# The causal layer with its key tiles in the order 0, 7, 1, 6, 2, 5, 3, 4, and its value products split by bank

## What is computed

```
x = layer_norm(hidden_states, ln1_w, ln1_b)
q = (x @ q_w + q_b) / math.sqrt(HEAD)      # 16 heads of 8 channels, 1024 tokens
k = x @ k_w + k_b
v = x @ v_w + v_b
scores = jnp.einsum('bhqd,bhkd->bhqk', q, k)
scores = jnp.where(causal, scores, neg)
attn = jax.nn.softmax(scores, axis=-1)
ctx = jnp.einsum('bhqk,bhkd->bhqd', attn, v)
```

## Time and profile before

| | |
|---|---|
| median of 3 runs | 3524.71 us (3523.38 to 3525.19) |
| profiled execution, its own time | 3526.23 us |
| its span, first to last instruction | 3524.5 us |
| TensorE busy, share of the span | 3180.8 us, 90% |
| VectorE, GpSimd, ScalarE busy | 70%, 53%, 48% |
| mean granted clock of TensorE | 0.937 of full speed |

### The profile page before, as it was taken

The page is one execution under the profiler, slowest core; times in us unless marked ns, Lnnn a source line. Parts: engine busy times, 40 slices in busy tenths (PEclk is TensorE's granted clock), DMA queues, the critical chain, the costliest instruction groups (busy, mean ns, idle before and its releaser), DMA issues. The chain is left out here.

```text
span 3524.5 us, 50933 instructions
## 1 busy us (share of the span) xinstructions
PE 3180.8 (90%) x18448; PEld 1856.2 (53%) x18448; DVE 2477.8 (70%) x4334; ACT 1689.5 (48%) x2048; POOL 1871.0 (53%) x1159
## 2 busy tenths in 40 slices
PE   5979797586448999999999999999999999999998
PEld 4757576332324555555555555555555555555445
DVE  6979798653258776877777787687777778767533
ACT  5758576243213444444444444444444444444442
POOL 3857575111222655655665565565566556556670
PEclk8989899567679999999999999999999999999998
DMA  1000000000410000000000000000000000000001
GB/s 62 1 1 1 1 1 1 12 1 1 140 22 3 1 1 1 4 1 1 1 4 1 1 4 1 1 4 1 1 1 4 1 1 2 1 1 1 1 1 35
DMA packets 20600, 28.47 MB, mean 8 GB/s; under 512 B 5124, under 2 KB 12424, under 8 KB 20232
## 3 DMA queue, kind: packets, MB, share of 16 engines
q1 hardware_dynamic: 19016, 22.09, 1.9%
q0 software_dynamic: 1344, 3.15, 0.3%
HBM read 21.56 MB, written 3.67 MB: 7 GB/s over the span
## 5 line engine op out<-in xcount | busy, mean ns | idle before, releaser
L2049 ACT ACTIVATE pair_probs<-banks 128x1024 f32<-128x1024 f32 (+1 forms) x944 | 965.5, 1026 | 1035.2 <-PE banks L1959 983.8
L2098 DVE TENSOR_REDUCE pair_peaks<-banks 128x1 f32<-128x512 f32 (+1 forms) x1800 | 1085.6, 665 | 271.4 <-PE banks L1941 257.6
L2191 POOL TENSOR_TENSOR pair_total_pool<-pair_total_pool,pair_probs 128x1536 f32<-128x1536 f32 x208 | 724.6, 3484 | 754.1 <-DVE pair_total L2112 748.9
L1982 PE MATMUL banks<-pair_probs,pair_values 128*64 128x512 f32 (+1 forms) x3776 | 872.8, 600 | 0.0
L1941 PE MATMUL banks<-pair_k_high,pair_q_high 64*128 64x512 f32 (+1 forms) x1920 | 568.0, 443 | 26.6 <-DVE pair_peaks L2091 14.0
L2180 POOL TENSOR_TENSOR pair_total_pool<-pair_total_pool,pair_probs 128x1024 f32<-128x1024 f32 x224 | 535.7, 2392 | 39.1 <-POOL pair_total_pool L2191 21.4
L2112 DVE TENSOR_TENSOR pair_total<-pair_total,pair_probs 128x512 f32<-128x512 f32 (+2 forms) x464 | 457.9, 987 | 94.5 <-ACT pair_probs L2049 69.3
L1982 PEld LDWEIGHTS banks<-pair_probs,pair_values 128*64 128x64 f32 (+1 forms) x3776 | 248.3, 136 | 472.6 <-issue 384.7
L1959 PE MATMUL banks<-pair_q_shift,pair_one_rows 64*128 64x512 f32 (+1 forms) x1888 | 475.4, 396 | 3.1 <-ACT pair_probs L2049 3.1
L1941 PEld LDWEIGHTS banks<-pair_k_high,pair_q_high 64*128 64x128 f32 x1920 | 263.1, 185 | 356.4 <-issue 211.9
L1959 PE MATMUL banks<-pair_q_high,pair_k_high 64*128 64x512 f32 (+1 forms) x1888 | 426.9, 391 | 0.0
(11 more groups left out here) (323 smaller groups left out, 3770.3 us busy)
## 6 DMA issues: line engine op xcount, KB each, us to landing
expert_w<-in_fc SPq DMA_DIRECT2D x32, 256.0 KB, 4.3
context_rows<-in_ctx SPq DMA_DIRECT2D x10, 320.0 KB, 6.4
dense_w<-in_We SPq DMA_DIRECT2D x2, 1024.0 KB, 9.2
experts_in<-expert_zeros SPq DMA_DIRECT2D x1, 1024.0 KB, 3.8
expert_b<-in_fc_b SPq DMA_DIRECT2D x2, 512.0 KB, 4.7
expert_rows<-experts_in SPq DMA_DIRECT2D x16, 64.0 KB, 2.0
experts_out<-expert_result POOLq DMA_DIRECT2D x4, 256.0 KB, 4.6
row_parameters<-in_rows SPq DMA_DIRECT2D x1, 896.0 KB, 8.4
```

The lines of the kernel that those rows point to most:

```text
L1982: last = pe.matmul(out[heads[head], :], values[0:n, ring_of(h // 2, i // 4), i % 4, heads[head]], probs_of(h, i)[0:n, head, :], start=i == ...
L2049: act.activation(probs_of(h, i)[0:n], slot(e)[0:n], ACT.Exp, scale=1.0 / 8.0).then_inc(S["expd"].sem, 1)
L2098: v.reduce_max(peaks[:, head, t, b:b + 1], fill_bank(f, head)[:, 0:width(b)], axis=AX).then_inc(S["peaked"].sem, 1)
L2191: pool.tensor_tensor(pooled[:], pooled[:], three, ALU.add).then_inc(S["pooled"].sem, 1)
```

## The change

The key tiles are taken in the order 0, 7, 1, 6, 2, 5, 3, 4. An add is split in two entries for tiles 0 to 3, one for each bank, each with its own semaphore count. The adds of a tile no longer stand behind the last unit of the next tile, but are spread between its units. The turns of the next group's queries and keys stand behind the first and the second score instead of ahead of all; the back of the group before stands behind the seventh score (in group 3 behind the first). The ring of `probs` and GpSimd's order go by the position of a tile in the new order.

```diff
+KEY_TILES = (0, 7, 1, 6, 2, 5, 3, 4)
+def banks_of(j):
+    return range(j // 4, 2)
...
-        for j in range(TT):
-            behind += [("score", g) + s for s in scores[j]]
-            if j:
-                behind.append(("add", g, j - 1))
         if g:
-            ahead.insert(min(4, len(ahead)), ("back", g - 1))
-        order += ahead[:2]
-        ahead = ahead[2:]
-        for entry in behind:
-            order.append(entry)
-            if entry[0] == "score" and ahead:
-                order.append(ahead.pop(0))
+            ahead.insert(min(6, len(ahead)), ("back", g - 1))
+        for n, j in enumerate(KEY_TILES):
+            adds = [("add", g, KEY_TILES[n - 1], bank) for bank in banks_of(KEY_TILES[n - 1])] if n else []
+            for m, piece in enumerate(scores[j]):
+                order.append(("score", g) + piece)
+                if ahead:
+                    order.append(ahead.pop(0))
+                while adds and (m + 1) * len(banks_of(KEY_TILES[n - 1])) >= len(scores[j]) * \
+                        (len(banks_of(KEY_TILES[n - 1])) - len(adds) + 1):
+                    order.append(adds.pop(0))
         order += ahead
         if g + 1 < NG:
             order.append(("shift", g + 1))
-        order += [("add", g, TT - 1), ("keep", g)]
+        order += [("add", g, KEY_TILES[-1], bank) for bank in banks_of(KEY_TILES[-1])] + [("keep", g)]
...
-                def add(g, j):
-                    wait(pe, "selected", TT * g + j + 1)
+                def add(g, j, bank):
+                    n = position[j]
+                    wait(pe, "selected", TT * g + n + 1)
                     wait(pe, "taken_scalar", last_score[g, j])
-                    if j == 0:
+                    if n == 0:
                         wait(pe, "kept", g)
-                    for bank in range(j // 4, 2):
-                        a, b = max(j * P, bank * 512), bank * 512 + 512
-                        for h in range(GROUP):
-                            last = pe.matmul(out[PART * h:PART * h + PART, bank, a - bank * 512:512],
-                                             values[:, j, g * GROUP + h, :], probs[:, j % 3, h, a - j * P:b - j * P],
-                                             start=j == 0, stop=j == 4 * bank + 3)
+                    a, b = max(j * P, bank * 512), bank * 512 + 512
+                    for h in range(GROUP):
+                        last = pe.matmul(out[PART * h:PART * h + PART, bank, a - bank * 512:512],
+                                         values[:, j, g * GROUP + h, :], probs[:, n % 3, h, a - j * P:b - j * P],
+                                         start=n == 0, stop=j == [c for c in KEY_TILES if bank in banks_of(c)][-1])
```

More of the change, by code:

```diff
@@ L908, in causal_order @@
         ahead = [("queries", g + 1), ("keys", g + 1)] + [("fill", g + 1) + f for f in fills] if g + 1 < NG else []
-        behind = []
-        for j in range(TT):
-            behind += [("score", g) + s for s in scores[j]]
-            if j:
-                behind.append(("add", g, j - 1))
-        if g:
-            ahead.insert(min(4, len(ahead)), ("back", g - 1))
-        order += ahead[:2]
-        ahead = ahead[2:]
-        for entry in behind:
-            order.append(entry)
-            if entry[0] == "score" and ahead:
-                order.append(ahead.pop(0))
+        if g:
+            ahead.insert(min(6, len(ahead)), ("back", g - 1))
[8 more added lines that the diff above has]
+                    order.append(adds.pop(0))
         order += ahead
@@ L966, in causal_attention @@
         fills_of_group = sum(unit[:2] == ("fill", 0) for unit in units)
+        adds = [unit for unit in order if unit[0] == "add"]
+        added = [max(n + 1 for n, unit in enumerate(adds) if unit[1:3] == (g, j)) for g in range(NG) for j in KEY_TILES]
+        position = {j: n for n, j in enumerate(KEY_TILES)}
         heads = lambda pair: slice(2 * pair, 2 * pair + 2)
@@ L1100, in exponential @@
                     wait_made(act, unit)
-                    if a == 0 and pair == 0:
-                        wait(act, "added", TT * g + j - 2)
-                    act.activation(probs[:, j % 3, heads(pair), a:b], slot(unit)[:, :, 0:b - a], ACT.Exp,
+                    n = TT * g + position[j]
+                    if a == 0 and pair == 0 and n >= 3:
+                        wait(act, "added", added[n - 3])
+                    act.activation(probs[:, position[j] % 3, heads(pair), a:b], slot(unit)[:, :, 0:b - a], ACT.Exp,
                                    scale=float(HD0) ** -0.5).then_inc(S["taken_scalar"].sem, 1)
@@ L1114, in _ @@
                     elif kind == "keep":
-                        wait(act, "added", TT * (g + 1))
+                        wait(act, "added", added[TT * g + TT - 1])
                         act.activation(out_sb[:].rearrange("p (b c) -> p b c", b=2), out,
@@ L1121, in _ @@
                 for g in range(NG):
-                    for j in range(TT):
+                    for n, j in enumerate(KEY_TILES):
                         wait(pool, "taken_scalar", first_score[g, j])
-                        diagonal = probs[:, j % 3, :, 0:P]
+                        diagonal = probs[:, n % 3, :, 0:P]
                         pool.affine_select(out=diagonal, in_=diagonal, compare_op=ALU.is_ge, fill=0.0, base=0,
```

## The result

The changed kernel takes 3541.89 us (median of 5 runs, 3537.74 to 3545.21) against 3524.71 for the kernel before on the same chip: a ratio of 1.0047, 95% interval 1.0036 to 1.0059. It is slower by 17.2 us, 0.47%, and lies 2.9 us above the upper end of the predicted range.

A forecast was written before the change was run, and what follows sets the result against it. The prediction took TensorE, busy for 90% of the span, to bound the kernel. Its terms +1.7 - 6.2 + 2.5 + 2.7 + 1.0 + 2.2 = +3.9 us took the median 3524.71 to 3528.6 us, range 3513 to 3539.

The forecast's parts named there:

- The clock stays low: Rival: no long product run, so no clock rise late in a group or in group 3; +14.0, 3538.7 us, chance 0.24.
- the prediction's own sign of being wrong: Whole forecast: wrong if TensorE's idle time falls over 9 us or the clock share moves over 0.08 either way.
- the first rival: The rival "Starvation ends": faster, 3511.6 us, chance 0.17.
- The clock, the step that failed: All four groups: small loss of full-clock time, +2.2 us, between bounds of 12.3 longer and 21.2 shorter.
- Group 3, +1.0: Last group, no fills: earlier first exponential, but waits at tiles 0 and 1 and a longer final chain; -1 to +4 us.
- The end of a group, +2.7: Ahead of the shift turn: fills left behind the last score make TensorE wait about 3.0 us, not 2.09; 3 x 0.9.
- Splitting the adds, +1.7: Products of tiles 0 to 3: 16 more runs at 0.20 us each, at most 3.2 us, half taken.
- What should have shown it: Sign for the split: ScalarE's idle times of 3 to 4 us ahead of an exponential gone, the largest under 2.5.
- Waits covered, -6.2: Tiles 3 to 5, groups 0 to 2: half adds between scores cover TensorE's 2.06 us a group of waits for exponentials.
- Start of a group, +2.5: First fill 7.0 us behind the shift turn, before 4.46; costs 1.0 each in groups 1 and 2, 0.5 in group 0.
- Starvation ends: Rival, groups 0 to 2: hidden half adds halve VectorE's idling at long tiles, 14.8 us less; 3511.6 us, chance 0.17.

The follow-up runs named there:

- turns alone: Kernel before with only the turns of queries and keys and the back moved behind the first scores and the seventh: 3536.24 us, 1.0035.
- split alone: Kernel before with only the adds split by bank and spread between the next tile's units: 3530.03 us, 1.0015.
- order and split: Changed kernel with the turns put back ahead of the first score: 3537.51 us, 1.0034.
- both repairs: Changed kernel with two fills behind each score of the last tile, and group 3 as in the kernel before: 3528.35 us, 1.0008.
- whole: New order: changed kernel with each tile's two banks again one unbroken run, 3536.44 us. Old order: the kernel before, 3524.71 us.
- joined: Adds of two tiles put together: in the kernel before (old order) 3530.67 us, in the changed kernel (new order) 3536.16 us.

## Why the prediction was wrong

The mechanism that decides was named as a rival, "The clock stays low", at 0.24, with 3538.7 us; the forecast of 3528.6 was 13.3 us too low. Its deciding condition, a mean clock below 0.60 in the four windows, is met (0.57, from 0.69), and so is the prediction's own sign of being wrong, a move of the clock by more than 0.08. The range ended at 3539, just above that rival's 3538.7 us, so anything that cost more than its price fell outside; at the other end it left out the first rival's 3511.6, which it was said mostly to take in. Step by step:

**The clock, the step that failed.** The term was +2.2, between 12.3 and -21.2. It was no sum of rows: I took a small loss because runs of turns and products at a group's start would stand in for the lost product runs. The clock is high at the start of group 1 for 6.9 us and of group 2 for 3.3 (788.5 to 791.8), but ScalarE is the fuller engine there. The turns alone, with all product runs as long as before, took groups 1 and 2 down to 0.53, the other way than this step had it. The row that the help of the turns rested on was also misread: at 728.20 the clock is up behind 16 transposes in all, not 24; the third eight start only then. The 4096 columns of products that ran at 1.00 before in groups 0 to 2 now run at 0.50: 4096 / 512 x 0.93 = 7.4 us. With the 2688 of group 3 it is the whole 12.3, less 0.5 for the 256 columns of tile 6, which are still at the full clock (0.64 us): 11.8 for the products alone where the term had 2.2. Products measured: +14.1 us of busy time, somewhat below 12.3 and the splits' own cost (16 x 0.23 = 3.7 at most) together, 16.0. The scores add 8.2 (43.6 before, 51.8 after by line) and the fills 3.5 (38.6 and 42.1); records of different lines overlap, so these don't sum to TensorE's 19.1. The bound of 12.3 also left these out: it priced the columns of the products alone.

**Group 3, +1.0, measured +7.4.** I looked for waits and sized them; idle time there is unchanged (8.5 and 8.4 us). The 7.4 is all busy time. The clock of this group stood in the clock term, and its bound there is 2688 / 512 x 0.93 = 4.9 us, for the columns of the products alone. Those that fell (4.4), the products from group 2 in this window (1.3) and four splits (0.9) make 6.6 of the 7.5 us of busy time.

**The end of a group, +2.7.** TensorE waits 3.4 to 4.1 us ahead of the shift turn, not 3.0; in sum 11.5 instead of 6.4 us, +5.1. Moving the fills forward gave back 6.7. The mechanism was right, the size about half.

**Splitting the adds, +1.7.** 0.23 us a split by the timeline, above the bound of 0.20: up to 3.7 if none of it is hidden (half of the prediction's 3.2 is 1.6, not 1.7). What should have shown it came out only in part: the longest idle time of ScalarE ahead of an exponential fell from 3.9 to 2.7 us, not below 2.5, and the sum of them rose.

**Waits covered, -6.2.** Fills waited 13.4 us for exponentials before and 8.5 now, -4.9. Right in kind and nearly in size, and undone elsewhere: the stage's idle time is the same.

**Start of a group, +2.5.** The first fill comes 6.5 us behind the shift turn (739.16 - 732.64), in the range of 6 to 7 named; in group 2 it is 7.4. Its cost was not measured by itself. The turns alone cost 11.5 us in all; of the stage's 13.7, 5.1 is the wait ahead of the shift and 11.0 is busy time, at a clock of 0.53 in groups 1 and 2, against 2.4 less of other waits.

**"Starvation ends".** Its condition, TensorE's idle time in groups 0 to 2 below 17 us, is far off: 26.8 instead of 26.3. The split alone and order and split came nearer, with 20.9 and 20.8, and show what the rival had left out: more than the idle time that went came back as busy time at the lower clock.

Put together with what was measured, groups 0 to 2 are +2.8 (12 splits) - 4.9 (waits) + 2.5 (start, as predicted) + 5.1 (end) = +5.5, and the 12.1 measured leave 6.6 for the clock, an estimate with an unmeasured term in it. By TensorE's own time it is 8.8: in groups 0 to 2 it is busy 11.6 us more, less 2.8 for the splits (10.1, if the 1.3 us of products that went to the next window are counted here). In the kernel with both repairs the same groups are 6.0 us above before, with 10.7 more of busy time and 4.7 less of idle. Of the loss of 17.2 us, what was shown by taking it away is the wait at the group's end (6.7) and group 3 (7.6), 13.5 with both at once. That the rest is the clock in groups 0 to 2 is argued from the rows, not shown by a kernel of its own: every kernel that raised the clock there changed the idle time too. Open is also what in the new order keeps the clock down. The length of the product runs goes with it in the new order (0.57 split, 0.64 whole, 0.66 joined); in the old order joined and whole adds are both at 0.69 and split ones at 0.58, the turns alone reach 0.59 without touching a run, and one list was granted two clocks ahead of the windows. The prediction should have said that its rows gave only the two bounds of this term, and opened its range to them.

## What to carry to other kernels

Where TensorE runs at a mean clock between its two levels, price each bit of its work at both levels before a reordering, and ask first which stretches are at the full clock now, what stands ahead of them, and whether the new order keeps that. Where the rows don't tell, the term is its two bounds and not a small number between them. Smaller pieces that feed the other engines sooner can lower TensorE's idle time and lengthen the stage all the same; here they helped only in the group that kept a high clock (group 3 in the old order). A high clock in a stretch where another engine is the busy one gives little.

## What the runs showed of the hardware

- With TensorE busy for 66.0 of 69.8 us (95%) on fills, scores, small transposes and split products, the granted clock was 0.50 throughout; the same kinds of instructions in the old order, with whole products, got 0.91 at 41.4 of 45.6 us (91%). The engine's share of busy time did not go with the clock.
- Nor did the work alone: 120 matmuls, the same in the same order in two kernels, were granted 0.50 over 36.9 us in one and 0.65 over 31.3 us in the other.
- Going from products to scores and back costs 0.23 us for each extra run (1.94 + 1.93 against 3.64 us), little beside what the lower clock cost.
- Spare transposes that only fill a wait left that wait as long (3.3 us in group 1) and still took 5.8 us off the changed kernel, nearly as much as removing most of the wait did (6.7). The Trainium skill (TensorE: Matmul & The Clock Gate, Part 4) says that the full clock doesn't engage for transposes, which don't count as busy in the same way. The runs are mixed on it: behind sixteen spare ones eight more took 1.09 us at a granted clock of 1.00, and with spare transposes the old order's clock rose from 0.65 to 0.91 in group 0, which both speak against it as a general rule; the new order's fell from 0.57 to 0.50.
